# Token scores of a cross-attention kernel: float32 products against masked keys, or f32r products of stacked halves

## The reference

```python
enc, ca = ctx[:, :124], ctx[:, 124:]
hs = mha(x @ Wq, enc @ Wk, enc @ Wv)                    # token attention: 124 keys
ca_q1 = einsum('btc,th->bch', ca, Wq_ca)[:, indices]    # 128 of 192 channels
ca_hs1 = mha(ca_q1, x, x)                               # channel attention
ca_hs2 = mha(ca_hs1 @ Wq, ca @ Wk_ca, ca @ Wv_ca)       # 4 keys
out = (hs + ca_hs2) @ Wout + b_out + x
# mha: softmax(q k^T / sqrt(40)) v per head
```

## Time and profile before

| | us |
|---|---|
| median of 3 runs | 245.86 |
| the runs | 246.77, 245.86, 245.26 |
| the profiled execution | 247.51 |
| its span | 245.7 |

### The profile page before, as it was taken

One profiled execution on the slowest core, in us unless ns is written; L12 is line 12 of the kernel. 1 busy time (PEld: TensorE's weight loads), 2 busy tenths in 40 slices (PEclk: granted clock), 3 DMA queues, 4 the chain that ended last, 5 costly groups with the idle time before them and its releaser, 6 DMA issues.

```text
span 245.7 us, 5529 instructions
## 1 busy us (share of the span) xinstructions
PE 224.6 (91%) x1756; PEld 208.4 (85%) x1770; DVE 175.7 (71%) x513; ACT 119.4 (49%) x311; POOL 52.6 (21%) x136
## 2 busy tenths in 40 slices
PE   0269999999999999999999999999999999999972
PEld 0269877989989998999899989998999989997971
DVE  2672997678876878587958696769777876877452
ACT  2425745244552664457355545463547552644640
POOL 3140070030322133022403060306030422010010
PEclk9999988999999999999999999999999999999998
DMA  7995023027956200520052003400242002000001
GB/s 220 271 253 182 4 60 108 3 60 145 202 109 191 61 0 29 181 70 1 16 166 91 0 0 118 128 28 0 60 153 60 0 32 75 0 4 27 27 0 56
DMA packets 11772, 19.60 MB, mean 80 GB/s; under 512 B 1437, under 2 KB 7933, under 8 KB 11757
## 3 DMA queue, kind: packets, MB, share of 16 engines
q1 hardware_dynamic: 11343, 18.30, 26.7%
q10 hardware_dynamic: 414, 1.11, 1.6%
HBM read 14.16 MB, written 2.62 MB: 68 GB/s over the span
## 4 chain that ended last, share of the span: by engine, by line
PE 83%; DVE 9%; issue 3%; DMA 2%; ACT 0%; DVEq 0%; SPq 0%; POOL 0%
PE bank_a L1069 15%; PE scores L1217 12%; PE bank_d L1245 11%; PE bank_d L1242 10%; PE bank_d L1300 7%; PE turned L1064 5%; PE bank_d L1069 5%; PE bank_a L1149 4%; PE scores L1189 3%; PE bank_d L1064 3%; PE bank_d L1113 3%; DMA caQ<-in_ca_picked 2%; PE turned L1205 2%; PE scores L1064 1%; PE bank_a L1064 1%
## 5 line engine op out<-in xcount | busy, mean ns | idle before, releaser
L817 DVE TENSOR_REDUCE neg_max<-scores 128x4 f32<-128x512 f32 (+1 forms) x64 | 41.3, 676 | 18.7 <-PE scores L1217 10.7
L622 ACT ACTIVATE probs<-scores,neg_max 128x124 f32<-128x124 f32 x128 | 34.3, 383 | 10.9 <-DVE neg_max L817 10.9
L1069 PE MATMUL bank_a<-xT_r,wq_r 128*120 128x256 f32 (+1 forms) x192 | 28.8, 303 | 10.6 <-DVE xT_r L732 10.6
L1069 PEld LDWEIGHTS bank_a<-xT_r,wq_r 128*120 128x120 f32 (+1 forms) x192 | 25.6, 195 | 10.7 <-issue 10.6
L1242 PEld LDWEIGHTS bank_d<-xg,probsT 128*128 128x128 f32 x256 | 30.1, 192 | 0.8 <-issue 0.5
L1245 PE MATMUL bank_d<-v_sb,probsT 124*128 124x41 f32 x256 | 30.7, 279 | 0.0
L1245 PEld LDWEIGHTS bank_d<-v_sb,probsT 124*128 124x128 f32 x256 | 30.4, 192 | 0.1
L1242 PE MATMUL bank_d<-xg,probsT 128*128 128x33 f32 x256 | 30.1, 272 | 0.4 <-DVE k_blocks L797 0.4
L611 ACT ACTIVATE probsT<-turned 128x512 f32<-128x512 f32 x32 | 17.4, 595 | 23.5 <-PE turned L1205 15.8
L1217 PE MATMUL scores<-k_blocks,qT 120*128 120x372 f32 (+2 forms) x96 | 24.0, 387 | 0.3
L516 ACT ACTIVATE probsT<-turned 124x512 f32<-124x512 f32 x32 | 17.4, 594 | 13.4 <-PE turned L1064 13.0
(11 more groups left out here) (127 smaller groups left out, 383.4 us busy)
## 6 DMA issues: line engine op xcount, KB each, us to landing
xT<-in_x_cols SPq DMA_DIRECT2D x8, 384.0 KB, 4.2
x_h<-in_x_heads SPq DMA_DIRECT2D x8, 360.0 KB, 3.6
x_sb<-in_x SPq DMA_DIRECT2D x8, 320.0 KB, 3.5
vw_stack<-vw_part SPq DMA_DIRECT2D x16, 160.0 KB, 3.6
out<-out_sb SPq DMA_DIRECT2D x16, 160.0 KB, 1.8
...
```

What stands on the lines that cost most here:

```text
L622: last = nc.scalar.activation(probs[:, h, 0:keys], scores[half][:, k * keys:(k + 1) * keys], ACT.Exp, bias=neg_max[:, h:h + 1])
L817: v.tensor_reduce(neg_max[:, 4 * half:4 * half + 4], scores[half][:, 0:4 * keys].rearrange("q (h k) -> q h k", h=4), AX.X, ALU.max, negate ...
L1069: ins = mm(dst, stationary(w, half, c), moving(w, half, c), start=first and i == 0, stop=last and i == len(steps) - 1)
```

## The change

- Queries and keys of a pair are split into an f32r high and low half in PSUM's layout: `q_parts`, `k_parts` (ScalarE the high halves, VectorE the low ones). 18 DMAs per pair, 9 for the queries and 9 for the keys, copy them so that each head has 120 rows: the queries high, high, low, the keys high, low, high (`q_stack`, `k_stack`, two of each). Heads at the same rows of their chunks lie side by side there, so that a DMA copies whole rows of 2 or 3 chunks. `token_scores` becomes one f32r product per head: 8 per batch, 124 columns each. The masked keys go.
- `QM` has its extra columns from row 96 on; a float32 copy of it (`qm_last`) feeds `MT`.
- In the pair, `KT01`, `QM`, `QT01` and `MT` come ahead of `turn_probs` of unit 2; `XG` waits for the low half of `QT01`, `MT` for that of `QM`.
- In the prologue `k2T` comes first, its masks go to VectorE; `G1` and `G2` go into the two banks for turned scores; the keys come ahead of the values. `wk_ca` is loaded ahead of `wk` and has a semaphore of its own. The halves of `Wout` are made in the first pair.
- `vw_stack` is laid out so that its DMAs copy whole rows of 5,120 bytes; they are issued within the first pair's list on SP.
- Some tiles share memory: `probs` with `wqT`, `probsT` with `wq`, `hs` and `by_head` with `wk` and `wv`, `out_sb` with `wout`.

The diff, cut:

```diff
-QW = HID + HT
+KL = HID - QC
+M_ROW = 96
+
+QW = QC + M_ROW + HT
 Q_CHUNKS = [slice(0, KC), slice(KC, QC), slice(QC, QW)]
-KL = QW - QC
+K_CHUNKS = [slice(0, KC), slice(KC, QC), slice(QC, HID)]
+
+
+Q_SLOTS, K_SLOTS = (0, 0, 1), (0, 1, 0)
+STACK = 16 * 9
+PLACE = [3 * (h % 3) + h // 3 for h in range(HEADS)]
...
-    return end * ["P3T"] + front * ["QM", "MT", "XG", "QT01", "V0", "V1"]
+    return end * ["P3T"] + front * ["QM", "QT01", "MT", "XG", "V0", "V1"]
...
-RING_A = Ring(["QM", "MT", "k2T", "QT01", "G0", "V0", "G2", "V1", "XG"],
+RING_A = Ring(["k2T", "QM", "G0", "MT", "QT01", "V0", "V1", "XG"],
               of_a(0, 1), of_a(1, 1), of_a(1, 0), ["P3T"])
-RING_D = Ring(["CA0", "MsT", "G1", "KT2", "KT01"],
+RING_D = Ring(["CA0", "MsT", "KT2", "KT01"],
...
-
-        k_blocks = sb("k_blocks", [KC, 2, 3, 2, KEYS])
-        k_last = sb("k_last", [KL, 2, 2, 2, KEYS])
+        q_parts = [sb(f"q_part{i}", [KC, NC, 2 * S], F32R) for i in range(2)]
+        k_parts = [sb(f"k_part{i}", [KC, NC, 2 * KEYS], F32R) for i in range(2)]
+        qm_last = sb("qm_last", [XP, 2 * S])
+
+        q_stack = [sb(f"q_stack{i}", [KC, HEADS, 2 * S], F32R) for i in range(2)]
+        k_stack = [sb(f"k_stack{i}", [KC, HEADS, 2 * KEYS], F32R) for i in range(2)]
...
+            def stack_heads(parts, slots, stack_sb, done):
+
+                for slot, part in enumerate(slots):
+                    for j in range(3):
+                        chunks = NC if j < HEADS - 6 else NC - 1
+                        sp.dma_start(
+                            stack_sb[D * slot:D * slot + D].bitcast(F32)[:, 3 * j:3 * j + chunks, :]
+                                .rearrange("p h n -> p (h n)"),
+                            parts[part][D * j:D * j + D].bitcast(F32)[:, 0:chunks, :]
+                                .rearrange("p c n -> p (c n)")).then_inc(done, 16)
...
-            sp.dma_start(wk[:, :, 0:HID], Wk).then_inc(loaded_wk, 16)
+            sp.dma_start(wk_ca[:], Wk_ca).then_inc(loaded_wk_ca, 16)
+            sp.dma_start(wk[:], Wk).then_inc(loaded_wk, 16)
             sp.dma_start(wv[:], Wv).then_inc(loaded_wv, 16)
...
+            sp.wait_ge(q_low, 2)
+            stack_heads(q_parts, Q_SLOTS, q_stack[0], q_stacked)
+            sp.wait_ge(d_drained, RING_D.no("prologue", "KT01")[0] + 1)
+            stack_heads(k_parts, K_SLOTS, k_stack[0], k_stacked)
...
+                if more:
+                    sp.wait_ge(d_drained, k_made)
+                    stack_heads(k_parts, K_SLOTS, k_stack[1 - at.par], k_stacked)
+                    sp.wait_ge(q_low, q_made)
+                    stack_heads(q_parts, Q_SLOTS, q_stack[1 - at.par], q_stacked)
+                if first:
+                    sp.wait_ge(d_drained, RING_D.no(at, "VW3")[0] + 1)
+
+                    stack_values(0)
+                if more and ahead:
                     sp.wait_ge(a_filled, xg_made)
                     load_xh(pair)
-
+                if first:
+                    stack_values(1)
...
+                    for slot, part in enumerate(VW_PART):
+                        sp.dma_start(
+                            vw_stack[HT * slot:HT * slot + HT].bitcast(F32)[:, 4 * r:4 * r + 4, :]
+                                .rearrange("p n h -> p (n h)"),
+                            vw_parts[part][HT * r:HT * r + HT].bitcast(F32)
+                                .rearrange("p n h -> p (n h)")).then_inc(vw_stacked[r // 2], 16)
...
+                act.wait_ge(loaded_own, 16)
+                if name == "G2":
+                    act.wait_ge(g_filled, 2)
+                    g_out(copy, turned[1], 2).then_inc(g2_made, 1)
+                else:
+                    g_out(copy, piece("prologue", name), 0).then_inc(a_drained, 1)
...
+                else:
+
+                    if at != "prologue":
+                        act.wait_ge(q_stacked, at.lin(STACK, STACK))
+                    if name == "QT01":
+                        ins = copy(q_parts[0][:, 0:2, :],
+                                   src[0:KC, :].rearrange("p (c n) -> p c n", c=2), SCALE)
+                    else:
+                        copy(qm_last[:, :], src[:, 0:2 * S], SCALE)
+                        ins = copy(q_parts[0][0:KL, 2, :], src[0:KL, 0:2 * S], SCALE)
...
+            def high_keys(at, name):
+
+                n, bank = RING_D.no(at, name)
+                act.wait_ge(d_filled, n + 1)
+                if at != "prologue":
+                    act.wait_ge(k_stacked, at.lin(STACK, STACK))
+                if name == "KT2":
+                    ins = copy(k_parts[0][0:KL, 2, :], bank_d[bank][0:KL, 0:2 * KEYS])
+                else:
+                    ins = copy(k_parts[0][:, 0:2, :], bank_d[bank][0:KC, 0:4 * KEYS]
+                               .rearrange("p (c n) -> p c n", c=2))
+                ins.then_inc(k_high, 1)
...
+            act.wait_ge(a_drained, RING_A.no("prologue", "k2T")[0] + 1)
             front("prologue", "QM")
+            setup("G0")
+            front("prologue", "MT")
+            act.wait_ge(loaded_wk, 16)
+            high_weight(wk, wk_r, CP - 1)
             act.wait_ge(loaded_wv, 16)
             high_weight(wv, wv_r, CP - 1)
-            front("prologue", "MT")
-            setup("k2T")
             front("prologue", "QT01")
-            setup("G0")
+            setup("G2")
+            high_keys("prologue", "KT2")
+            high_keys("prologue", "KT01")
             values(piece("prologue", "V0"), 0, 0)
-            setup("G2")
             values(piece("prologue", "V1"), 0, 1)
-            act.wait_ge(loaded_wout, 16)
-            high_weight(wout, wout_r, XC - 1)
             front("prologue", "XG")
...
+                if more:
+                    high_keys(at, "KT2")
                 exps_turned(unit(at, 1))
                 exps(unit(at, 2), KEYS)
                 if more:
+                    high_keys(at, "KT01")
                     front(at, "QM")
+                    front(at, "QT01")
+                    front(at, "MT")
                 turned_copy(unit(at, 2), KEYS)
                 if more:
-                    front(at, "MT")
-                    front(at, "XG")
                     exps3(at)
                 exps(unit(at, 3), KEYS)
-                if not more:
+                if more:
+                    front(at, "XG")
+                else:
                     exps3(at)
-                if more:
-                    front(at, "QT01")
                 turned_copy(unit(at, 3), KEYS)
...
+            def keys_ca():
+                n, bank = RING_A.no("prologue", "k2T")
+                dve.wait_ge(a_filled, n + 1)
+                for j in range(3):
+                    last = v.tensor_scalar(
+                        k2_blocks[:, :, :, T * j:T * j + T],
+                        bank_a[bank][0:KC, 0:NC * B * T].rearrange("p (c b t) -> p c b t", c=NC, b=B),
+                        hmask[:, 0, j, 0:1], None, ALU.mult)
+                last.then_inc(a_drained, 1)
...
+            def g_heads(src, r):
+                heads_in = 3 if r < 2 else 2
+                for c in range(NC):
+                    width = T * (3 if c < 2 else 2)
+                    rows, shape = src[0:KC], [KC, B, heads_in, width]
+                    last = v.tensor_tensor(
+                        g_blocks[:, r, :, 0:heads_in, 3 * T * c:3 * T * c + width],
+                        rows[:, c * B * 3 * T:c * B * 3 * T + B * width]
+                            .rearrange("p (b n) -> p b n", b=B).unsqueeze(2).broadcast_to(shape),
+                        hmask[:, 0, 0:heads_in, 0:1].unsqueeze(1).broadcast_to(shape), ALU.mult)
+                return last
...
+            def low_q(at, name):
+
+                n, bank = RING_A.no(at, name)
+                dve.wait_ge(a_drained, n + 1)
+                c = slice(0, 2) if name == "QT01" else slice(2, 3)
+                rows = KC if name == "QT01" else KL
+                v.scalar_tensor_tensor(q_parts[1][0:rows, c, :],
+                                       bank_a[bank][0:rows, 0:(c.stop - c.start) * 2 * S]
+                                       .rearrange("p (c n) -> p c n", n=2 * S), SCALE,
+                                       q_parts[0][0:rows, c, :], ALU.mult, ALU.subtract) \
+                    .then_inc(q_low, 1)
...
+                if name in ("KT01", "KT2"):
+                    dve.wait_ge(k_high, (1 if name == "KT2" else 2) if at == "prologue"
+                                else at.lin(2, 3 if name == "KT2" else 4))
+                    if name == "KT01":
+                        ins = v.tensor_tensor(k_parts[1][:, 0:2, :], src[0:KC, 0:4 * KEYS]
+                                              .rearrange("p (c n) -> p c n", c=2),
+                                              k_parts[0][:, 0:2, :], ALU.subtract)
+                    else:
+                        ins = v.tensor_tensor(k_parts[1][0:KL, 2, :], src[0:KL, 0:2 * KEYS],
```

(72 more changed lines are left out.)

127 lines of the change are left out of this document (56 added, 71 removed).

## The result

The changed kernel takes 250.86 us (median of 4 runs, 249.11 to 252.89), the kernel before 245.73 (245.26 to 246.77). The ratio is 1.017, 95% interval 1.012 to 1.022: slower by 1.7%, where 4% faster was forecast. Of the other profiles only the one of the run with TensorE's idle time filled has it as long.

The account below looks back on a forecast made before the run. TensorE's own instructions were taken to set the pair's length (25.73 us). The terms -13.0 (token scores) + 1.4 (waits) + 0.4 (start) + 1.0 (first stacks) = -10.2 us gave a median of 235.6 us, 8-in-10 range 230.8 to 243.

Parts of the forecast that it names:

- The token scores: Token scores on TensorE: eight f32r matmuls at 110 ns, 0.88 us a group for 1.69, times 16 = 13.0 us gained.
- cheap loads: Rival for the token scores: an f32r load costs what a bf16 one does, 0.46 us a group, 231.0 us; chance 0.06.
- no gain: Rival for the token scores: 124 columns cost 207 ns, so a group stays as dear, 248.6 us; chance 0.03.
- The hand-overs: Waits in each pair for `m_stack` and `m_rows`: 0.2 us charged for both, 1.4 us in 7 pairs.
- the 24.4 of the rivals: Pair length in us that the rival with transfers slower than the other work compared its 29.9 us with.
- The transfers at the start: First pair's stack copies at 185 GB/s, 1.5 us to land: there at about 38.9 us, token scores wait 1.0 us.
- The start: Prologue in its new order: queries free at about 25.5 us, `MsT` waits about 2.7, first pair begins 0.4 us later.
- The clock: Half clock between 36 and 38 us in the start: no gain given, 1.7 us kept either way.
- Fewer DMA engines: Rival: 40-row transfers run at 10/16 rate, hidden in pairs, 6 us late at the start, 243.1 us; chance 0.12.
- Transfers become the bound: Rival for every pair: below 97 GB/s stack transfers make the kernel slower; at 80 GB/s 274 us; chance 0.05.
- Hand-overs: Rival: ScalarE's queue in mid-pair or `m_rows` comes later, 1.0 us more per pair, 242.6 us; chance 0.14.

## Why the prediction was wrong

**The token scores: right.** 0.88 us a group was forecast, 0.84 measured: an f32r matmul of 124 columns with its own load goes at 105 ns, a float32 one of 33 columns at 107, as assumed. So the rivals *cheap loads* and *no gain* fall.

**The hand-overs: in the right places, too small.** The groups save 1.68 us a pair, the pair is 1.12 shorter: 0.56 us went, where 0.2 was charged. 0.15 of it is the wait in front of the pair's first token scores (for the low half of the hidden, a place not named), 0.14 each are `MsT` (0.38 for 0.24 us) and the channel scores (0.62 for 0.48), whose operands now come just as TensorE asks, and the rest is hundredths of several groups. The sum's own terms make a pair 24.3 us (25.73 - 1.62 + 0.2, not the 24.4 of the rivals); 24.61 is 0.3 above it, 2.1 us in seven pairs. VectorE (166.3 us busy against 168) and ScalarE (126.7 against 130) came out near what was worked out.

**The transfers at the start: the step that failed.** The prediction had SP's issue time in hand (0.35 to 0.8 us each) and used it only where it was hidden, as 8 to 19 us of a pair. For the start it took bytes over 185 GB/s, and 1.5 us to land, for which no row stands (1.85 us measured): stacks there at 38.9 us, 1.0 us waited (25.5 + 10.4 + 1.5 is 37.4; the 38.9 has the 256 KB of `ctxT` ahead of them at the same rate). Measured, eighteen issues of 0.75 us with the gap are 13.6 us, behind 27.77 that is 41.4, with the landing 43.2 us, and the wait was 3.9 us. Half of the delay is this step by itself: from the prediction's own 25.5 us, eighteen issues at 0.75 us and its 1.5 us to land give 40.6 us and a wait of 2.6. The upper end of its own 0.35 to 0.8 us would have told it., 0.78 us an issue, would have come near too, but by luck: that row stands at a full DMA share, and in the changed kernel the same 160 KB, as whole rows, are issued in 0.59 us each.

**The start: the queries came 2.3 us later than worked out** (27.8 for 25.5 us). The wait for `MsT` was 3.9 us for 2.7, and the loss of 0.4 at the first `scores_turned` was 2.5. This is a term summed up over three engines with no row of the new order, and it was given no bound of its own. No experiment got it back: in all of them the first `scores_turned` starts at 32.8 to 35.1 us, for 30.8 in the kernel before. What of the new order costs it stays open.

**The clock: a term put at nothing.** "I give no gain for it and keep 1.7 us either way" took the one stretch at half clock in the earlier trace rows for the measure. The changed kernel's profile has stretches at 43 to 50, 67 to 70 and 237 to 244 us besides the one in the start; filling the idle time ahead of the first token scores took the first of these away and gave some 3.5 us back. The prediction charged the waits and nothing for what they do to the work behind them.

**The rivals.** *Fewer DMA engines* had the size of the delay at the start nearly right, 6 us late (43.35 us for 37.36), and the engines right, about ten at a time, but not the cause: with a third to a half of the bytes the keys come at the same time. *Transfers become the bound* was wrong; the steady pairs hide them. *Hand-overs* took a third of the 1.0 us more per pair that it asked for. No rival named the issue time at the start or the clock behind a wait, and the forecast's low price for both is why only 0.07 was left for slower.

The sum by stretches, in us of the profiled spans:

| stretch | forecast's terms | measured |
|---|---|---|
| start | +0.4 | +2.5 |
| to the first token scores | +1.0 | +3.5 |
| first pair from there | -1.4 | +4.3 |
| six pairs | -8.5 | -6.2 |
| last pair | -1.6 | +1.3 |

In the first pair 3.1 us are the clock behind the stacks (gone when the idle time was filled). Set against the saving of 1.6 us, 2.8 more went there: new waits of 0.9 and 0.5 us, 0.9 us of turned probabilities at half clock, and the hand-overs. In the last pair the saving is eaten by the late stretch at half clock of this execution; in the profiles that lack it, the last pair is 24.9 to 26.7 us for 27.9 before. Why it comes is open.
